# A Mamba scan kernel: where the drive of every second pair of states is made, and by which engine

## The reference, cut to what matters

```python
h = _rmsnorm(x, norm_w)                       # x is layer-normed first
u, z = split(h @ in_proj_w)                   # (512, 512) each
u = silu(causal_depthwise_conv(u, conv_w, conv_b))
xdbl = u @ x_proj_w                           # 64 columns for dt, 16 for B, 16 for C
dt = softplus(xdbl[..., :64] @ dt_proj_w + dt_proj_b)
def step(hst, inp):
    dA = exp(dt_t[..., None] * A)
    dBu = dt_t[..., None] * B_t[:, None, :] * u_t[..., None]
    hst = dA * hst + dBu
    y = einsum('bdn,bn->bd', hst, C_t)
y = (y + u * D) * silu(z)
out = x + y @ out_proj_w
```

## Time and profile before

| what | before |
|---|---|
| median of three runs | 3050.72 us |
| the profiled execution, its own time | 3049.55 us |
| its span, first to last instruction | 3047.7 us |
| TensorE busy | 2680.0 us, 88% of the span |
| VectorE busy | 2345.8 us, 77% |
| ScalarE busy | 1847.0 us, 61% |
| GpSimd busy | 1824.2 us, 60% |
| mean granted TensorE clock | 0.949 |

### The profile page before, as it was taken

How to read it: one execution, slowest core, us unless ns; L and a number is a source line. 1 busy time by engine, 2 the same in 40 slices (tenths; PEclk the granted TensorE clock), 3 DMA queues, 4 the chain that set the end, 5 groups by cost and what they waited for, 6 DMA issues and landing times. The chain is left out here.

```text
span 3047.7 us, 48452 instructions
## 1 busy us (share of the span) xinstructions
PE 2680.0 (88%) x17374; PEld 2139.6 (70%) x17374; DVE 2345.8 (77%) x2432; ACT 1847.0 (61%) x2523; POOL 1824.2 (60%) x1211
## 2 busy tenths in 40 slices
PE   5999995795389999999999999999999999985793
PEld 4877874563158788788787787787887877874562
DVE  6888874463259898898988998988989989895563
ACT  3565562252178677776776776676777767761451
POOL 1221220454148778777777787787877877784454
PEclk8999998798599999999999999999999999997896
DMA  1121213323222021120220210202202202103423
GB/s 48 63 62 41 62 49 73 108 77 89 77 70 63 15 84 43 42 84 8 77 85 1 84 59 26 84 14 72 84 2 83 70 15 77 43 29 80 119 77 100
DMA packets 137178, 186.01 MB, mean 61 GB/s; under 512 B 27848, under 2 KB 112712, under 8 KB 136968
## 3 DMA queue, kind: packets, MB, share of 16 engines
q1 hardware_dynamic: 129480, 162.68, 17.3%
q0 software_dynamic: 7488, 20.46, 2.6%
HBM read 141.12 MB, written 41.98 MB: 60 GB/s over the span
## 5 line engine op out<-in xcount | busy, mean ns | idle before, releaser
L1287 POOL TENSOR_TENSOR m_state<-m_state,m_c_all 128x1024 f32<-128x1024 f32 x512 | 1204.5, 2366 | 358.8 <-DVE m_state L1379 357.7
L1379 DVE TENSOR_TENSOR_SCAN m_state<-m_decay,m_ps_d 128x1024 f32<-128x1024 f32 x512 | 1161.9, 2278 | 149.9 <-issue 88.8
L1447 ACT ACTIVATE m_decay<-m_dt,m_aneg 128x511 f32<-128x511 f32 x1024 | 657.6, 710 | 27.4 <-DVE m_state L1379 26.6
L1671 PEld LDWEIGHTS m_ps_d<-m_bdiag,m_duT 128*128 128x128 f32 x4096 | 491.8, 193 | 109.8 <-issue 77.3
L1671 PE MATMUL m_ps_d<-m_bdiag,m_duT 128*128 128x128 f32 x4096 | 508.1, 278 | 33.3 <-DVE m_state L1379 23.7
L1684 PE MATMUL m_ps_y<-m_ident,m_state 128*128 128x128 f32 x4096 | 534.2, 274 | 2.8 <-POOL m_state L1287 2.5
L1684 PEld LDWEIGHTS m_ps_y<-m_ident,m_state 128*128 128x128 f32 x4096 | 464.7, 142 | 8.4 <-POOL m_state L1287 7.3
L1356 DVE TENSOR_TENSOR m_duB<-m_duT,m_ps_i 128x1024 f32<-128x1024 f32 x256 | 306.0, 1195 | 7.7 <-ACT m_duT L1475 7.7
L1669 PEld LDWEIGHTS m_ps_d<-m_ident,m_duB 128*128 128x128 f32 x2048 | 235.6, 141 | 76.8 <-issue 70.8
L1669 PE MATMUL m_ps_d<-m_ident,m_duB 128*128 128x128 f32 x2048 | 265.8, 273 | 7.1 <-DVE m_state L1379 7.0
L1585 PE MATMUL m_ps_f<-m_hT,m_win 128*128 128x512 f32 x512 | 248.7, 610 | 18.9 <-DVE m_dt L1323 16.6
(11 more groups left out here) (194 smaller groups left out, 4417.4 us busy)
## 6 DMA issues: line engine op xcount, KB each, us to landing
m_c_all<-m_c_rows SPq DMA_DIRECT2D x128, 512.0 KB, 5.3
out<-m_xw SPq DMA_DIRECT2D x32, 512.0 KB, 3.1
f_y_rows<-f_y_sb SPq DMA_DIRECT2D x46, 256.0 KB
a_xin<-x SPq DMA_DIRECT2D x16, 512.0 KB, 4.8
a_xres<-x SPq DMA_DIRECT2D x16, 512.0 KB, 5.7
x<-a_xout SPq DMA_DIRECT2D x16, 512.0 KB, 3.3
m_xin<-x SPq DMA_DIRECT2D x16, 512.0 KB, 5.3
m_xw<-out SPq DMA_DIRECT2D x16, 512.0 KB, 5.4
```

Source lines behind the costliest of these rows:

```text
L1287: nc.gpsimd.tensor_tensor(s, s, c_all[:, n, :, :], ALU.mult).then_inc(weighed, 1)
L1379: nc.vector.tensor_tensor_scan(state[:, r, :, :].rearrange("p n t -> p (n t)"), decay[:, r, :, :].rearrange("p n t -> p (n t)"), ps_d[i % ...
L1447: ins = nc.scalar.activation(decay[:, r, j, 1:S], dt_sb[:, c, 1:S], ACT.Exp, scale=aneg[:, c, n:n + 1])
L1671: ins = nc.tensor.matmul(drive_t, duT[:, c, t, :], bdiag[:, n // 2, TT * j + t, :], start=True, stop=True)
```

## The change: what it does

1. TensorE makes the drive of odd pairs only, always in `ps_d[1]`. For even pairs VectorE writes the drive itself into `ps_d[0]`: dt*u of the group, channels on partitions, in a PSUM bank `ps_u`, times B spread over the partitions in `b_all`. It does so in turn i (even) for pair i+2, and in turn 30 for pair 0 of the next item.
2. ScalarE copies dt*u to `ps_u` (`put_du`) in turns 5, 13, 21 and 29.
3. SyncE stores the rows of B beside those of C (eight small stores for four) and loads B for the four even n, 512 KB each (`b_pair`), behind the loads of C for n = 0, 2, 4 and 6.
4. The diagonal blocks are no longer made by VectorE: those of n = 1 and 3 by GpSimd in turns 26 and 28 of the item before, those of n = 5 and 7 by ScalarE in turns 0 and 3, eight copies of the identity with a scale each.
5. `dt_sb` and `duT` have two buffers where they had four.
6. Moved: O(0) from TensorE's turn 16 to 17, X, Y(1) with DU(3), B, DT(0) and O(1) one turn later each; on VectorE the residual sums from 17 and 23 to 18 and 24, the statistics from 14 to 11, the relu of dt(0) from 23 to 24; on GpSimd the finish of dt(0) from 23 to 24 and `norm` (eleven small steps) from 15 to 13; on ScalarE the copies of DU(3), X, B and the first softplus one turn later.

```diff
@@ -1026,12 +1027,12 @@
-        16: [("O", 0, -1)],
-        18: [("X", 0, 1)],
-        19: [("Y", 1, 0), ("DU", 3, 0)],
-        20: [("B", 0, 1)],
-        21: [("DT", 0, 1)],
-        22: [("O", 1, -1)],
+        17: [("O", 0, -1)],
+        19: [("X", 0, 1)],
+        20: [("Y", 1, 0), ("DU", 3, 0)],
+        21: [("B", 0, 1)],
+        22: [("DT", 0, 1)],
+        23: [("O", 1, -1)],
         24: [("Z", 0, 1)],
         25: [("Z", 1, 1)],
...
-        dt_sb = sb("dt", [P, CT, S])
+        dt_sb = sb("dt", [P, DR, S])
         du_sb = sb("du", [P, 2, S])
-        duT = sb("duT", [P, CT, TT, P])
+        duT = sb("duT", [P, DR, TT, P])
...
-        duB = sb("duB", [P, SR, 2, TT, P])
+        b_all = sb("b_all", [P, NP // 2, 2, S])
...
-        ps_i = psum("ps_i", [P, S])
+        ps_u = psum("ps_u", [P, S])
...
+            def b_pair(m):
+
+                sp.dma_start(b_all[:, m, :, :], bc_rows[0, 4 * m:4 * m + 2, :].partition_broadcast(P))\
+                    .then_inc(b_loaded[m], 16)
 
             def emit(st):
                 if st.has(0):
                     c_pair(st, 0, NP - 2)
+                    b_pair(NP // 2 - 1)
...
                     for q in range(Q):
-                        sp.dma_start(c_rows[G * q:G * q + G, :], xd[bass.ds(R + N + q, G, step=Q), :])\
-                            .then_inc(c_stored, 16)
+                        for j in range(2):
+                            sp.dma_start(bc_rows[j, G * q:G * q + G, :], xd[bass.ds(R + N * j + q, G, step=Q), :])\
+                                .then_inc(c_stored, 16)
...
-                    sp.wait_ge(c_stored, 16 * Q * (b + 1))
+                    sp.wait_ge(c_stored, 32 * Q * (b + 1))
                     if st.has(0):
                         sp.wait_ge(weighed, drained)
                     for n in range(NP - 2):
                         c_pair(st, 1, n)
+                        if n % 2 == 0:
+                            b_pair(n // 2)
...
                 if k >= 2 or st.has(o - 1):
                     pool.wait_ge(du_full, n - 1)
-                nc.gpsimd.tensor_tensor(du_sb[:, k % 2, :], dt_sb[:, k, :], u_sb[h][:, k, :],
+                    pool.wait_ge(du_put, n - 1)
+                nc.gpsimd.tensor_tensor(du_sb[:, k % 2, :], dt_sb[:, k % DR, :], u_sb[h][:, k, :],
                                         ALU.mult).then_inc(du_ready, 1)
+
+            def diagonal(st, o, n):
+
+                h, b = st.half(o), st.item(o)
+                pool.wait_ge(bt_ready, b + 1)
+                if st.has(o - 1):
+                    pool.wait_ge(drive_full, UN // 2 * b - NP // 2 + n // 2 + 1)
+                nc.gpsimd.tensor_tensor(bdiag[:, n // 2, :, :], id_sb[:, :].unsqueeze(1).to_broadcast([P, 2 * TT, P]),
+                                        bt[h][:, 2 * n:2 * n + 2, :].rearrange("p n t -> p (n t)").unsqueeze(2)
+                                        .to_broadcast([P, 2 * TT, P]), ALU.mult).then_inc(b_made[n // 2], 1)
...
-                    if i in (23, 30) and st.has(1):
-                        finish_dt(st, 1, (23, 30).index(i))
-                    if i == 15 and st.has(2):
+                    if i in (24, 30) and st.has(1):
+                        finish_dt(st, 1, (24, 30).index(i))
+                    if i in (26, 28) and st.has(1):
+                        diagonal(st, 1, i - 25)
+                    if i == 13 and st.has(2):
                         norm(st)
 
...
+                if k >= DR or st.has(o - 1):
+                    dve.wait_ge(decay_ready, UN * b + NP * (k - DR + 1))
+                nc.vector.scalar_tensor_tensor(out=dt_sb[:, k % DR, :], in0=f_bank("DT", k)[:, :], scalar=0.0,
...
+                    dve.wait_ge(du_put, CT * b + c + 1)
+                if c == 0:
+                    dve.wait_ge(b_loaded[n // 2], 16 * (b + 1))
+                if i >= 2 or st.has(o - 1):
+                    dve.wait_ge(scanned, UN * b + i - 1)
+                nc.vector.tensor_tensor(ps_d[0][:, :, :], ps_u[:, :].unsqueeze(1).to_broadcast([P, 2, S]),
+                                        b_all[:, n // 2, :, :], ALU.mult).then_inc(scaled, 1)
 
...
-                        dve.wait_ge(drive_full, g + 1)
+                        dve.wait_ge(drive_full if i % 2 else scaled, UN // 2 * st.item(0) + i // 2 + 1)
...
-                    if i % 2 and i + 3 < UN and st.has(0):
-                        scale(st, 0, i + 3)
-                    if i % 2 and i + 3 >= UN and st.has(1):
-                        scale(st, 1, i + 3 - UN)
+                    if i % 2 == 0 and i + 2 < UN and st.has(0):
+                        scale(st, 0, i + 2)
...
-                    if i == 0 and st.has(0):
-                        diagonal(st, 0, NP - 1)
...
-                    if i in (17, 23) and st.has(-1):
-                        b, v = st.item(-1), (i - 17) // 6
+                    if i in (18, 24) and st.has(-1):
...
-                    if i == 14 and st.has(2):
+                    if i == 11 and st.has(2):
...
-                    if i in (23, 30) and st.has(1):
-                        dt_relu(st, 1, (23, 30).index(i))
-                    if i == 25 and st.has(1):
-                        dve.wait_ge(bt_ready, st.item(1) + 1)
-                        nc.vector.tensor_copy(ps_bt[st.half(1)], bt[st.half(1)][:, :, :]).then_inc(bt_put, 1)
-                    if i in (26, 28, 30) and st.has(1):
-                        diagonal(st, 1, i - 25)
+                    if i in (24, 30) and st.has(1):
+                        dt_relu(st, 1, (24, 30).index(i))
+                    if i == 30 and st.has(1):
+                        scale(st, 1, 0)
...
+                if c >= DR or st.has(o - 1):
+                    act.wait_ge(drive_full, UN // 2 * b + NP // 2 * (c - DR + 1))
+                nc.scalar.activation(duT[:, c % DR, :, :].rearrange("p t d -> p (t d)"), f_bank("DU", c)[:, :],
+                                     ACT.Copy).then_inc(duT_ready, 1)
+
+            def put_du(st, o, c):
+
+                b = st.item(o)
+                act.wait_ge(du_ready, CT * b + c + 1)
+                if c or st.has(o - 1):
+                    act.wait_ge(scaled, UN // 2 * b + NP // 2 * c)
+                nc.scalar.activation(ps_u[:, :], du_sb[:, c % 2, :], ACT.Copy).then_inc(du_put, 1)
+
+            def diagonal(st, o, n):
+
+                h, b = st.half(o), st.item(o)
+                act.wait_ge(bt_ready, b + 1)
                 if st.has(o - 1):
-                    act.wait_ge(drive_full, UN * b - UN + NP * (c + 1))
-                nc.scalar.activation(duT[:, c, :, :].rearrange("p t d -> p (t d)"), f_bank("DU", c)[:, :],
-                                     ACT.Copy).then_inc(duT_ready, 1)
+                    act.wait_ge(drive_full, UN // 2 * b - NP // 2 + n // 2 + 1)
+                for j in range(2):
+                    for t in range(TT):
+                        ins = nc.scalar.activation(bdiag[:, n // 2, TT * j + t, :], id_sb[:, :], ACT.Copy,
+                                                   scale=bt[h][:, 2 * n + j, t:t + 1])
+                ins.then_inc(b_made[n // 2], 1)
...
-                    if i in (2, 12, 20) and st.has(0):
-                        to_duT(st, 0, 1 + (2, 12, 20).index(i))
-                    if i == 19 and st.has(1):
+                    if i in (2, 12, 21) and st.has(0):
+                        to_duT(st, 0, 1 + (2, 12, 21).index(i))
+                    if i == 20 and st.has(1):
...
-                            act.wait_ge(c_stored, 16 * Q * b)
+                            act.wait_ge(c_stored, 32 * Q * b)
...
-                    if i == 21 and st.has(1):
+                    if i == 22 and st.has(1):
                         b = st.item(1)
                         act.wait_ge(b_full, b + 1)
                         if st.reuses(1):
-                            act.wait_ge(b_ready, NP // 2 * (b - 1))
-                            act.wait_ge(scaled, UN // 2 * (b - 1))
+                            for n in range(2):
+                                act.wait_ge(b_made[n], b - 1)
...
-                    if i in (22, 29) and st.has(1):
-                        softplus(st, 1, (22, 29).index(i))
+                    if i in (23, 29) and st.has(1):
+                        softplus(st, 1, (23, 29).index(i))
+                    if i in (5, 13, 21) and st.has(0):
+                        put_du(st, 0, 1 + (5, 13, 21).index(i))
                     if i == 27 and st.has(1):
                         to_duT(st, 1, 0)
+                    if i == 29 and st.has(1):
+                        put_du(st, 1, 0)
+                    if i in (0, 3) and st.has(0):
+                        diagonal(st, 0, 5 if i == 0 else 7)
...
-                if n == 0:
+                if n == 1:
                     pe.wait_ge(duT_ready, CT * b + c + 1)
-                if n % 2 == 0:
-                    pe.wait_ge(scaled, UN // 2 * b + i // 2 + 1)
-                elif c == 0:
```

(14 more changed lines are left out.)

46 lines of the change are left out of this document (12 added, 34 removed).

## The result

The median of four runs is **3023.8 us** (3022.2 to 3024.8) against 3049.7 us for the kernel before on the same chip: ratio 0.992, interval 0.990 to 0.9934. The direction was right, but the forecast was 95 us less and the change gave 26; the time lies outside the range.

The account below looks back on a forecast made before the run. After the change VectorE binds (104.5 us an item, TensorE 103.2); with 8.7 us of waiting 113.2, 6.5 less than 119.7. Fifteen items save 98 us, 2 come back: 3049.55 to 2953.6, as median 2955 us, range 2890 to 3010.

Parts of the forecast that it names:

- VectorE's own work: VectorE's busy time an item: 106.6 us, less 4.8 for diagonals, plus 2.7 for dearer multiplications, makes 104.5 us.
- the gate rows: Profile rows of VectorE's two gate steps, from which the multiplication's wait for its scan was priced at 0.13 us.
- ScalarE, GpSimd, SyncE: Added work an item: ScalarE to 94.7 us, GpSimd to 98.6 us, SyncE's loads of B at cost 0.
- TensorE: TensorE's busy time an item: 117.1 us less 13.9 for 16 transposed drives, makes 103.2 us.
- What is left waiting: Walk through one item listing VectorE's remaining waits: 8.7 us together where there were 12.4.
- VectorE's term: VectorE's need of 104.5 us an item, including 0.13 us for each multiplication's wait for its scan.
- terms (1) to (6): VectorE waits, us: drive 9 1.9; decay 11 0.8; drive 17 1.6; turn-25 y 0.9; scan 28 0.4; dt*u copy 2.6.
- Small ones, 0.5: Last entry in the list of an item's remaining waits: unnamed small waits, 0.5 us together.
- B: Rival: ScalarE's copies (0.50 us) or GpSimd's diagonals (4.7 us) take over as limit; 3020 us, chance 0.14.
- A: Rival: everything packs, TensorE early enough that most waits vanish, item 107.5 us; 2870 us, chance 0.12.
- C: Rival: slower, VectorE's multiplication into PSUM costs like the scan, 2.28 us; 3145 us, chance 0.07.
- D: Rival: no change, scans didn't wait for the transposes and decay waits take the freed time; 3051 us, chance 0.03.

Follow-up runs that it names:

- gate 21: Changed kernel with VectorE applying the gate of group 1 in turn 21 instead of 20: 2997.7 us, ratio 0.984.
- all three kernels: Changed kernel with gate 21 (2997.7 us); that with DT(2), DT(3) one TensorE turn later (3002.1); that with ScalarE's SiLU one turn later too (3000.7).

## Why the prediction was wrong

- **VectorE's own work: right.** The multiplication takes 1.233 us (taken: 1.24) and starts 2.31 us after its scan (1258.77 to 1261.08; foretold 2.3); before the change one that didn't wait for the scan ahead of it started 2.19 us after it (median). So the wait is paid, about 0.12 us, as the gate rows said. The Trainium skill, "VectorE: DVE Perf Modes", section "The DRAIN you can't avoid", has the semaphore cost nothing extra, measured there on copies; that is not borne out here. VectorE is busy for 103.4 us an item, and with 0.9 us of gaps ahead of the multiplications it comes to 104.3 against 104.5.
- **ScalarE, GpSimd, SyncE: priced high enough.** A ScalarE copy of 128 columns costs 4.9 / 16 = 0.31 us by busy time (taken: 0.34; the 390 ns in its row are one copy's duration, and neighbours overlap); a GpSimd diagonal 1.91 (taken: 2.37, that of the weighing). ScalarE's diagonals are hidden (3022.0 us without them), and B's loads made nothing wait. The estimate of 4.7 us for 16 copies from the Trainium skill, "VectorE: DVE Perf Modes", section "The TRN2 errata", is borne out by the 4.9 us of the trace.
- **TensorE: 2 us too low, and more with the clock.** 105.4 us in the ninth item against 103.2; 107.6 in the mean of the fifteen, 102 us of which are at half clock.
- **What is left waiting: this step failed.** It put 8.7 us of waiting where 15.0 were measured, 14.1 without the gaps that VectorE's term has. An item was to fall by 6.5 us and fell by 1.8 (120.3 to 118.5): 4.7 x 15 = 70 us, the 69 between 2955 and 3024. The last item (100.2 us for 97.8, foretold +1) and the start (no change, foretold +1) missed by 1 us each, in opposite directions, and what follows the last scan was 2.7 us shorter. Held against the list in the fourth item: (a) terms (1) to (6) were all there, 9.5 us in place of 8.2, and larger but for the copy: scans 9 and 17 2.10 each, scan 11 1.0, y at 25 1.1, scan 28 0.8, the copy 2.35. (b) The gate of turn 20, 1.5 us, was not on it: I costed Y(1)'s move by the y reading that it helps and not by the gate that stands behind it; gate 21 shows 26 us. (c) "Small ones, 0.5" were 2.5. (d) The loop's jump, 2.7 us at five of the ends, was not on it either; written out, the loop gives 16 us back.
- **The reading behind that step.** I took each stall for one engine's queue, and expected TensorE's slack to shorten it. TensorE has next to none in turns 4 to 10 and 13 to 20, which hold the convolutions; it lies in turns 11 and 12 and from 21 on, where VectorE waits mostly for other things. At scans 9 and 17 three things stand behind the second V (drive, decay, the reading of y), and order moves the wait from one to the next: 13.5 to 13.6 us for turns 8 to 10 in all three kernels. What shortened it was less work there: 55 us for half a convolution. Front turns moved from the full turns into the idle ones weren't tried.
- **The base.** The list began from 12.4 us of named waits in the fourth item; the fifteen have 13.8 in the mean.
- **Rivals.** B came nearest in time (3020), by luck: its dear copies (0.50 us) and diagonals (4.7 us) took 0.31 and 1.91 us, and ScalarE without its diagonals gains nothing. A and C are excluded, by the waits and by the multiplication's 1.233 us. D was nearer to the truth than its 0.03: waits did take the place of the transposes, and what was gained fits VectorE's diagonals (4.8 us an item less to do, 2.9 in all).
